# A recurrence, two attentions and a mixture of experts on one core: weights loaded a stage ahead, an uneven split of the GRU's tail, a reordered filter stage

## What is computed

```python
# 1. GRU over the 512 positions, start state = cond
gi = x_t @ W_ih + b_ih;  gh = h @ W_hh + b_hh
r, z = sigmoid(i_r + h_r), sigmoid(i_z + h_z);  n = tanh(i_n + r * h_n)
h = (1 - z) * n + z * h
# 2. differential causal attention, 16 heads: attn1, attn2 (rotary, softmax)
# 3. filter over the positions, norm per head, output product, residual
a = irfft((rfft(attn1) - lam * rfft(attn2)) * filt)
a = a * rsqrt(mean(a*a) + eps) * rms_weight * (1 - LAMBDA_INIT);  x = x + a @ Wout
# 4. norm with gain and shift from cond, full attention, o + o @ W_out
xn = rms_norm(x) * g_norm * (1 + cond @ W_emb[:, :D] + b) + (cond @ W_emb[:, D:] + b')
# 5. top 6 of 64 experts per token, capacity 128; shared expert; sum; residual
```

## Time and profile before

| | us |
|---|---|
| median of 3 runs | 4526.82 |
| lowest, highest | 4515.19, 4535.55 |
| the profiled execution's own time | 4517.86 |
| its span | 4516.1 |
| PE busy in the span | 3734.1 (83%) |
| DVE, ACT, POOL busy | 2242.8, 1318.2, 527.0 |
| HBM read, written | 147.89 MB, 62.92 MB |

### The profile page before, as it was taken

The page is one execution under the profiler, slowest core; times in us unless marked ns, Lnnn a source line. Parts: engine busy times, 40 slices in busy tenths (PEclk is TensorE's granted clock), DMA queues, the critical chain, the costliest instruction groups (busy, mean ns, idle before and its releaser), DMA issues. The chain is left out here.

```text
span 4516.1 us, 167227 instructions
## 1 busy us (share of the span) xinstructions
PE 3734.1 (83%) x68303; PEld 2458.8 (54%) x68364; DVE 2242.8 (50%) x6299; ACT 1318.2 (29%) x4238; POOL 527.0 (12%) x1085
## 2 busy tenths in 40 slices
PE   7888888888888888887899998477999979688850
PEld 3277777777777777776444443243333334344420
DVE  2155555555555555554677777133666643222224
ACT  1023333333333333332344444122444411011100
POOL 0000000000000000000222232000000004300026
PEclk9999999999999999999999999688999979899975
DMA  2150000000000000001111110201111111288769
GB/s 70 29 177 0 0 0 0 0 0 0 0 0 0 0 0 0 0 0 39 42 42 49 49 33 17 81 25 50 49 65 49 49 65 57 74 261 261 261 181 202
DMA packets 144489, 256.71 MB, mean 57 GB/s; under 512 B 25943, under 2 KB 76247, under 8 KB 142388
## 3 DMA queue, kind: packets, MB, share of 16 engines
q1 hardware_dynamic: 102004, 159.95, 10.8%
q0 software_dynamic: 21248, 53.30, 4.4%
q10 hardware_dynamic: 21184, 42.76, 3.1%
HBM read 147.89 MB, written 62.92 MB: 47 GB/s over the span
## 5 line engine op out<-in xcount | busy, mean ns | idle before, releaser
L305 PE MATMUL gru_pr<-gru_whh,h 128*4 128x128 f32 x16384 | 543.7, 273 | 230.6 <-DVE h L396 230.6
L305 PEld LDWEIGHTS gru_pr<-gru_whh,h 128*4 128x4 f32 x16384 | 388.4, 87 | 373.9 <-DVE h L396 367.8
L305 PE MATMUL gru_pz<-gru_whh,h 128*4 128x128 f32 x16384 | 541.3, 273 | 1.3 <-issue 1.3
L305 PE MATMUL gru_pn<-gru_whh,h 128*32 128x128 f32 x16384 | 541.7, 273 | 0.0
L305 PEld LDWEIGHTS gru_pn<-gru_whh,h 128*32 128x32 f32 x16384 | 458.4, 110 | 1.3
L305 PEld LDWEIGHTS gru_pz<-gru_whh,h 128*4 128x4 f32 x16384 | 438.3, 87 | 9.3 <-issue 1.4
L376 DVE STREAM_TRANSPOSE gru_tr<-gru_pr 128x128 f32<-128x128 f32 x512 | 162.3, 317 | 380.0 <-PE gru_pr L305 380.0
L340 ACT ACTIVATE gru_rn<-gru_pre 128x16 f32<-128x16 f32 x512 | 118.4, 231 | 700.4 <-DVE gru_pre L378 700.4
L280 POOL COPY gru_pick<-ident 128x4 f32 x512 | 96.5, 188 | 1685.2 <-PE gru_pz L296 1679.9
L891 DVE TENSOR_REDUCE da_mx<-da_ps 128x2 f32<-128x1024 f32 (+3 forms) x256 | 201.2, 817 | 133.5 <-PE da_ps L582 133.5
L389 DVE STREAM_TRANSPOSE gru_tz<-gru_pz 128x64 f32<-128x64 f32 x1024 | 194.6, 229 | 120.2 <-PE gru_pz L305 120.2
(11 more groups left out here) (266 smaller groups left out, 5457.4 us busy)
## 6 DMA issues: line engine op xcount, KB each, us to landing
ex_wg<-in_L_ffn_gate_up_proj SPq DMA_DIRECT2D x64, 768.0 KB, 4.7
ex_wd<-in_L_ffn_down_proj ACTq DMA_DIRECT2D x64, 384.0 KB, 6.7
xg<-gru_zeros SPq DMA_DIRECT2D x4, 4096.0 KB
da_hb<-wide SPq DMA_DIRECT2D x16, 1024.0 KB, 4.7
fa_hb<-xnT SPq DMA_DIRECT2D x16, 1024.0 KB
ex_xg<-xg ACTq DMA_DIRECT2D x64, 256.0 KB, 6.0
eo<-ex_eo POOLq DMA_DIRECT2D x64, 256.0 KB, 5.4
da_wg<-ahead SPq DMA_DIRECT2D x48, 256.0 KB, 4.9
```

The lines of the kernel that those rows point to most:

```text
L305: last = nc.tensor.matmul(rows(j), of(c), whh[:, c, g, j, :], start=(c == 0 and start), stop=(c == KD - 1))
```

## The change

1. A second lasting tile, `ahead2`. Each stage finds its large weights loaded by the stage before: W_ih spreads from `ahead` (four places) into `ahead2`; W_hh and the start state are loaded during the gate inputs, by SP; the first attention's weights go to `ahead2`, its `hb` and the filter matrix to `ahead`; W_qkv to `ahead2`; W_out, the gate and the shared gate matrix are loaded at the end of the full attention; the first four experts' `wg` at the end of routing.
2. Gate inputs: PE transposes batch 0 only, then starts its gates as soon as W_ih is spread; the transposes of batch b+1 stand between the gates 3 to 6 of batch b. The loops over batches are written out.
3. GRU tail: the two halves become a part of one chunk and a part of three. PE waits before chunks 0 and 1.
4. Filter stage as a pipeline over batches: the filter products run one batch ahead, the turning of the normed rows and the output products one behind; the embedding product is computed with the condition as the stationary operand, its inputs loaded as rows and transposed by PE; `y` has two places, the output products two banks of their own.
5. Routing waits first for nothing, then for two matrices.

```diff
 def gate_inputs_stage
-                if k >= 2:
-                    pool.wait_ge(w_spread, 3 * (k - 1))
-                pool.dma_start(wraw[:, k % 2, :], W_ih[k * P:(k + 1) * P, :]).then_inc(w_in[k % 2], 16)
+                pool.dma_start(wraw[:, k, :], W_ih[k * P:(k + 1) * P, :]).then_inc(w_in[k], 16)
...
+            sp.wait_ge(w_in[KD - 1], 16)
+            sp.dma_start(xin[:, 1, :, :], x[1].rearrange("(tt p) d -> p tt d", p=P)).then_inc(x_in[1], 16)
+            for jj in range(KD):
+                for c in range(KD):
+                    sp.dma_start(t.hin[32 * jj:32 * jj + 32, c, :],
...
+            sp.wait_ge(w_spread, 3 * KD)
...
+                for c in range(KD):
+                    sp.dma_start(whh[32 * jj:32 * jj + 32, c, :, :, :].rearrange("i g j f -> i (g j f)"), rows[:, c, :]).then_inc(whh_in, 16)
...
+            for k in range(KD):
+                transpose_x(0, k)
+            pe.wait_ge(w_spread, 3 * KD)
             for b in range(B):
+                pe.wait_ge(xT_ready, (b + 1) * KD)
                 for c in range(NG):
+                    gate(b, c)
+                    if b < B - 1 and c in (3, 4, 5, 6):
+                        transpose_x(b + 1, c - 3)
 def gru_stage
-        HALVES = (0, 1)
-        HC, HS = KD // 2, ST // 2
+        PARTS = (slice(0, 1), slice(1, KD))
...
-                    if s is not None and c % HC == 0:
-                        pe.wait_ge(h_ready, s * 2 + (c // HC + 1))
+                    if s is not None and c < 2:
+                        pe.wait_ge(h_ready, s * 2 + (c + 1))
...
-                for half in HALVES:
-                    nc.vector.transpose(tz[:, half * HC:(half + 1) * HC, :].rearrange("p c x -> p (c x)"),
-                                        pz[:, par, half * 64:(half + 1) * 64]).then_inc(tz_done, 1)
+                for part in PARTS:
+                    nc.vector.transpose(tz[:, part, :].rearrange("p c x -> p (c x)"),
+                                        pz[:, par, part.start * 32:part.stop * 32]).then_inc(tz_done, 1)
 def diff_attention_stage
+            sp.dma_start(t.filt[:], t.const["filt"].rearrange("(s p) t -> p s t", p=P)).then_inc(filt_in, 16)
             sp.sem_inc(v_done, 2)
             with sp.Fori(0, B) as b:
 def filter_stage (SP)
+            sp.dma_start(condr[:], cond).then_inc(small_in, 16)
+            for n, vec in enumerate((b_emb[0:D], b_emb[D:2 * D], g_norm)):
+                sp.dma_start(bgr[n * KD:(n + 1) * KD, :], vec.rearrange("(k p) -> k p", p=P)).then_inc(small_in, 16)
...
+            sp.dma_start(rmsw[:].rearrange("p o (h d) -> p (o h) d", h=H), rms_row.broadcast_to([P, H, DH])).then_inc(rms_in, 16)
+            sp.dma_start(wemb[:], W_emb.rearrange("(k p) n -> p k n", p=P)).then_inc(wemb_in, 16)
+            sp.dma_start(wout[:], Wout.rearrange("(k p) n -> p k n", p=P)).then_inc(wout_in, 16)
 filter_stage (PE)
+            apply_filter(0)
...
+            apply_filter(1)
+            pe.wait_ge(wemb_in, 16)
...
+            turn(y[:, 0, :, :], y_ready, 0)
...
+            times_wout(0, moved)
+            for i in range(2, B + 1):
+                if i < B:
+                    apply_filter(i)
+                turn(y[:, (i - 1) % 2, :, :], y_ready, i - 1)
+                moved = tuple(used)
+                turn(xn, normed, i - 2)
+                times_wout(i - 1, moved)
+            turn(xn, normed, B - 1)
 filter_stage (DVE)
+            dve.wait_ge(rms_in, 16)
+            nc.vector.tensor_scalar(rmsw[:], rmsw[:], 1.0 - LAMBDA_INIT, None, ALU.mult).then_inc(rms_ready, 1)
+            dve.wait_ge(rms_ready, 1)
+            norm_heads(0)
...
+            residual_and_norm(0)
+            for i in range(2, B + 1):
+                if i < B:
+                    norm_heads(i)
+                keep_y(i - 1)
+                keep_normed(i - 2)
+                residual_and_norm(i - 1)
+            keep_normed(B - 1)
 def route_stage (SP, after the four batches' loads)
+            for u in range(t.EU):
+                sp.dma_start(t.ex_wg[:, u, :, :], gate_up[u].rearrange("(p k) i -> p k i", p=P)).then_inc(S["wg_in"], 16)
 def expert_stage
-            for u in range(U):
-                load_gate_up(sp, u, u)
```

More of the change, by code:

```diff
@@ L97, in _, with gate @@
+            def gate(b, c):
+                m = b * NG + c
+                if m >= 4:
+                    pe.wait_ge(gi_even if c % 2 == 0 else gi_odd, (m - 4) // 2 + 1)
+                col = GATES[c // KD] * D + (c % KD) * P
+                for k in range(KD):
+                    last = nc.tensor.matmul(pg[:, c % 4, :], wih[:, k, col:col + P], xT[:, b, k, :], start=(k == 0), stop=(k == KD - 1))
+                last.then_inc(gi_psum, 1)
             pe.wait_ge(ident_in, 16)
+            for k in range(KD):
+                transpose_x(0, k)
@@ L1064, in _, with times_wout @@
-                pe.wait_ge(yT_act, b * 2 + 2)
-                pe.wait_ge(yT_dve, b * 2 + 2)
+                        last = nc.tensor.transpose(to[:, tt * P:(tt + 1) * P], rows[:, tt, k * P:(k + 1) * P], t.ident[:])
+                    last.then_inc(turned, 1)
+            def times_wout(b, moved):
+                pe.wait_ge(act_moved, moved[0])
+                pe.wait_ge(dve_moved, moved[1])
                 for tt in range(TT):
+                    if b * TT + tt >= 2:
+                        pe.wait_ge(x1_ready, b * TT + tt - 1)
@@ new lines, in _ @@
+            pe.wait_ge(cond_ready, 2)
+            to = bank(1)
+            for k in range(KD):
+                for n in range(2):
+                    last = nc.tensor.matmul(to[32 * n:32 * n + B, :], condT[:, k, :], wemb[:, k, n * D:(n + 1) * D],
+                                            start=(k == 0), stop=(k == KD - 1))
+            last.then_inc(turned, 1)
+            turn(y[:, 0, :, :], y_ready, 0)
+            moved = tuple(used)
+            pe.wait_ge(emb_ready, 2)
+            to = bank(1)
@@ new lines, in _ @@
+            for k in range(KD):
+                last = nc.tensor.transpose(to[:, k * NR:(k + 1) * NR], embr[:, k * P:(k + 1) * P], t.ident[0:NR, 0:NR])
+            last.then_inc(turned, 1)
+            pe.wait_ge(wout_in, 16)
+            times_wout(0, moved)
[3 more added lines that the diff above has]
+                turn(y[:, (i - 1) % 2, :, :], y_ready, i - 1)
+                moved = tuple(used)
+                turn(xn, normed, i - 2)
+                times_wout(i - 1, moved)
@@ L1097, in _, with keep_normed @@
                 for k in (0, 2):
-                    act.wait_ge(yT_psum, b * KD + k + 1)
-                    nc.scalar.activation(yT[:, k, :], pt[:, k, :], ACT.Copy).then_inc(yT_act, 1)
+                    act.wait_ge(turned, seen[0] + k + 1)
+                    nc.scalar.activation(yT[:, k, :], pt[:, 0, :], ACT.Copy).then_inc(act_moved, 1)
+                seen[0] += KD
+            def keep_normed(b):
+                for k in (0, 2):
+                    act.wait_ge(turned, seen[0] + k + 1)
+                    nc.scalar.activation(t.xnT[:, b, k, :], pt[:, 0, :], ACT.Identity,
+                                         bias=shift[:, k, b:b + 1], scale=gain[:, k, b:b + 1]).then_inc(act_moved, 1)
+                seen[0] += KD
```

452 lines of the change are left out of this document (232 added, 220 removed).

## The result

The changed kernel took 4380.48 us (median of 4 runs, 4376.34 to 4388.93), the kernel before, on the same chip, 4525.65 (4 runs, 4515.19 to 4535.55): ratio 0.9682, 95% interval 0.9656 to 0.9708. Forecast were 4389 and faster. The profiled execution took 4376.34 us with a span of 4374.5, 141.5 less than the 4517.86 before; the sum of the prediction was -137.5.

The account below looks back on a forecast made before the run. Eight stages between barriers were costed separately, the recurrence largest (1897 of 4516 us, PE waiting 0.45 us a step for the new state). Terms -14 -14 -25 +3 -67 -11 -9.5 = -137.5 gave a median of 4389; range 4340 to 4440.

Parts of the forecast that it names:

- Gate inputs: First stage: with W_ih in four places, gates start at 18 us instead of 32, z products at about 137.5: -14 us.
- Opening of the recurrence: Start of the recurrence stage: weights and state have already arrived, only DVE's setup and a bias row remain: -14 us.
- The tail of a step: Recurrence, 512 steps: short first part saves 0.07 us, chunk 1 comes 0.02 late, so 0.05 a step: -25 us.
- Rival (a): Recurrence: the uneven tail gives nothing, as chunk 1 is late by what part 0 gained; -112 us in all, chance 0.22.
- First attention: First attention stage: the 1 MB filter matrix, queued ahead of the first head loads, delays PE: +3 us.
- Filter stage: Filter stage: earlier start and batches overlapped at 37 us each, with the rms weight landing at 2865: -67 us.
- Rival (b): Filter stage: the rms weight is quick by itself, slowed only by element-wise loads; 20 us more gained, -157 in all, chance 0.14.
- Rival (c): Filter stage: batches don't overlap and still take 48 us each; about -40 there, -117 to none else, -110 in all, chance 0.06.
- Routing: Routing stage: weights are already in, so the first product comes at 3666 instead of 3676.65: -11 us.
- Experts: Expert stage: PE starts 4.5 us earlier and some 5 us of waiting before expert 1 go: -9.5 us.
- Rival (e): Routing and expert stages: loads ahead are only moved, so both gain nothing; -117 us in all, chance 0.05.
- Rival (d): Recurrence: PE's waits make the clock grant fall in a fifth of the 512 steps, +330 us, 4720; chance 0.03.

## Why the prediction was right

**The reading by stage** held: every stage but the experts' came within 3.1 us of its term, and those that no edit reached stayed within 3.1 us.

**Gate inputs**, -14 against -14.5: start at 18.96 for 18, z products at 137.34 for 137.5. The half clock that was priced at the start of the gates (1 to 3 us) did not come: the grant is 1.00 over the whole stage. That makes up for the late start. That W_ih would be bounded by its bytes, and that x of batch 1 behind it would still be in time, both hold; the run with all transposes first shows what is lost otherwise, 12 to 13 us.

**Opening of the recurrence**, -14: PE's first product is 14.0 us sooner.

**The tail of a step**, -25 against -24.3 (by undoing it alone; -26 against the kernels of that run's own chip) and -25.2 (1875.3 against 1914.5, less 14.0). Both terms of it are measured apart: 0.07 gained is 0.072, 0.02 late at chunk 1 is 0.025. Rival (a), no gain, is out, by 24 us against a scatter of 2 us among the eight recurrences with this tail (1873.5 to 1875.3). That so fine a difference could be forecast is due to the size scaling read from two forms of the same instruction; the three-part tail then recovers just the 0.025.

**First attention**, +3 against +2.6, and -4.3 when the filter matrix is moved behind.

**Filter stage**, -67 against -64.1. The mechanism was right in each step (gap, its end by DVE, 37 us a batch, 22.8 to the last output products), and the term that was mis-sized is the rms weight. The sum took 23 us, as 34.6 less the 12.5 of the load ahead of it. For the kernel before that was a good reading: there its pieces start from 2849.75 to 2873.68, in 23.9 us. Its DMA view, in the stretch from 2837 to 2880 us:

```profile
DMA  0589999999992000000000000000000012747799
GB/s 8 67 200 402 328 413 385 438 396 419 415 388 81 11 11 8 11 11 8 11 11 11 8 11 11 10 9 11 11 8 11 11 11 9 7 4 63 272 377 400
```

In the changed kernel the same pieces took 29.3 us, 14.3 ns for each and not 11.7. The step that failed is the one that carried the duration of the load over unchanged to its new place at the head of the queue; why it is slower there is open. It began 2 us sooner than forecast and was in 4 us later, and batch 1's products started 2.6 us later than forecast, which is the miss. Rival (b), the weight quick by itself, is out in the form given; but its other half, that without it the stage gains another 20, was measured at 23 to 25. Rival (c), no overlap, is out by the 37 us.

**Routing**, -11 against -12.2, on two chips.

**Experts**, -9.5 against -19.2 in the pair of profiles. The step "experts 1 to 3 don't wait" holds but for 1.47 us before expert 1; the opening gives 7.5, and the difference of the means is 11. The rest of the 19.2 is the stage's own scatter, which one profile of before did not show. So it is in part luck that the sum met the measured 141.5: with 11 for the experts it would have been 133. Rival (e), loads only moved, said that routing and experts gain nothing. Routing gained 12 us on each of two chips. For the experts the two medians of one chip (4414.94 against 4408.89) don't decide, since the intervals of the ratios overlap; the lead that is still 5.3 us at half of the stage speaks against it.

**Rival (d)**, the clock, did not show: the grant is 1.00 over the 1857 us of the steps.

## What to carry to other kernels

When a transfer is read from a profile, ask of its source as well as of its pieces: a row broadcast to many places in small pieces costs by the piece (about 14 ns here) and blocks its queue, and the cure is one piece per partition and an engine to spread it. An uneven split of a tail pays if the first part is as small as the consumer's first need and each later part arrives while the one before is consumed; the idle time of the consumer's first group and the growth of its busy time price the two sides apart. Where a stage's time scatters by more than an edit is worth, compare openings in the timeline, the time at a fixed point inside the stage, and means over all kernels that share it, not one pair.

## What the runs showed of the hardware that was not expected

2048 reads of the same 128 bytes took about 30.8 us, with 10 GB/s in the queue, against less than 3 (issued at 2787.49, used at 2790.44) for 2048 reads of 128 bytes from distinct places. The price is one for each read: 14.3 ns with 2048 of them, 14.2 with 128; in the kernel before, behind 4 MB of other loads, 11.7.

On three other chips the consumers of PE's products in the routing stage, DVE or ACT alike, got PE's signal up to 9.9 us late while POOL issued its scatter (96 instructions of 0.98 us, 0.3 apart), up to 8.2 in the kernel before. With the half clock behind it the stage took 280 to 293 us in the changed kernel and its variants, not 259. On the first chip it did not happen at all. The traces differ in one thing more: those of the first chip hold 1536 updates of the semaphore that tells of the scatter's landings, those of the other three 390 to 453. The cause is open.
